# A scan kernel's projections hooked to steps of the second branch, one direction a pass ahead, with B and C spread by DMA

## The reference, cut to what matters

```python
def _mamba(x, Win, convw, convb, Wx, Wdt, bdt, Alog, Dp, Wout):
    xz = x @ Win
    xi, z = jnp.split(xz, 2, axis=-1)
    xi = jax.nn.silu(_causal_dwconv(xi, convw, convb))
    xdbc = xi @ Wx                                  # 8 + 16 + 16 columns
    dt_in, Bm, Cm = ...
    dt = jax.nn.softplus(dt_in @ Wdt + bdt)
    A = -jnp.exp(Alog)
    y = _selective_scan(xi, dt, A, Bm, Cm, Dp)      # h = exp(dt A) h + dt u B;  y = sum_s h C + u D
    return y * jax.nn.silu(z) @ Wout
...
x = layernorm(x + two_directional_mamba(x))         # mamba forward and backward, norms, a small FFN
x = layernorm(x + gated_ffn(x))                     # a*b, two 512x512 layers with gelu, 512 to 128
x = layernorm(x + attention(x))                     # 8 heads, 2 KV heads, latent 32, causal
x = layernorm(x + mixture_of_8_experts(x, top 2))
```

## Time and profile before

| | |
|---|---|
| median of 3 runs | 2261.87 us (2260.26 to 2264.23) |
| the profiled execution | 2270.57 us, its span 2268.8 us |
| busy PE, DVE, ACT, POOL | 1876.0, 1533.2, 1075.0, 791.3 us |
| granted TensorE clock, mean | 0.894 |

### The profile page before, as it was taken

How to read it: one execution, slowest core, us unless ns; L and a number is a source line. 1 busy time by engine, 2 the same in 40 slices (tenths; PEclk the granted TensorE clock), 3 DMA queues, 4 the chain that set the end, 5 groups by cost and what they waited for, 6 DMA issues and landing times.

```text
span 2268.8 us, 28172 instructions
## 1 busy us (share of the span) xinstructions
PE 1876.0 (83%) x8672; PEld 870.7 (38%) x8672; DVE 1533.2 (68%) x2151; ACT 1075.0 (47%) x1486; POOL 791.3 (35%) x632
## 2 busy tenths in 40 slices
PE   5432988899788988899788987899888997897888
PEld 2200334443334434353344433353344433443435
DVE  2988288856798378874888468882888567982214
ACT  2332573537445473546545473545735374452122
POOL 0445053432445044441545133540534324450001
PEclk9555999899899998899899998999998998988999
DMA  6987386706675195824866085823867067740000
GB/s 196 232 204 181 74 215 158 182 15 159 171 187 118 41 213 151 194 49 111 205 166 154 6 217 135 215 70 89 205 161 181 11 161 172 187 111 5 0 1 5
DMA packets 102673, 301.18 MB, mean 133 GB/s; under 512 B 15216, under 2 KB 31232, under 8 KB 102528
## 3 DMA queue, kind: packets, MB, share of 16 engines
q1 hardware_dynamic: 98304, 297.20, 53.7%
q10 hardware_dynamic: 4224, 2.10, 0.3%
HBM read 280.39 MB, written 18.87 MB: 132 GB/s over the span
## 4 chain that ended last, share of the span: by engine, by line
PE 56%; DVE 16%; issue 9%; ACT 8%; DMA 7%; POOL 3%; SPq 1%; DVEq 1%; POOLq 0%; ACTq 0%
PE ps_pair L659 22%; PE ps_in L582 8%; PE ps_pair L756 7%; DVE sb_hst L1197 6%; PE ps_pair L744 5%; PE ps_pair L823 5%; DMA sb_ring<-spread_dram 4%; DMA spread_dram<-sb_dd 2%; PE ps_y L611 2%; POOL sb_hc L1405 2%; PE ps_pair L777 2%; DVE ps_in L1190 2%; PE ps_y L582 2%; ACT sb_ring L891 1%; PE ps_pair L759 1%
## 5 line engine op out<-in xcount | busy, mean ns | idle before, releaser
L1405 POOL TENSOR_TENSOR sb_hc<-sb_hst,sb_crep 128x512 f32<-128x512 f32 x512 | 655.3, 1282 | 721.7 <-DVE sb_hst L1197 700.5
L1197 DVE TENSOR_TENSOR_SCAN sb_hst<-sb_ring,ps_in 128x512 f32<-128x512 f32 x512 | 620.3, 1213 | 0.0
L891 ACT ACTIVATE sb_ring<-sb_ring,sb_A 128x512 f32<-128x512 f32 x512 | 350.9, 714 | 271.1 <-DMA sb_ring<-spread_dram 269.9
L1190 DVE TENSOR_TENSOR ps_in<-sb_ring,ps_brow 128x512 f32<-128x512 f32 x512 | 354.8, 693 | 18.0 <-PE ps_y L582 4.1
L611 PE MATMUL ps_y<-sb_hc,sb_const 128*32 128x512 f32 x1024 | 154.6, 679 | 131.5 <-POOL sb_hc L1405 121.5
L659 PE MATMUL ps_pair<-sb_xn,sb_ew 128*128 128x512 f32 x512 | 251.5, 638 | 8.6 <-DVE sb_h L1349 7.3
L744 PE MATMUL ps_pair<-sb_h,sb_g 128*128 128x512 f32 (+3 forms) x512 | 197.9, 525 | 29.3 <-DVE sb_nmax L1297 28.1
L1395 POOL TENSOR_TENSOR sb_dd<-sb_dd,sb_texp 128x512 f32<-128x512 f32 x32 | 40.8, 1274 | 506.5 <-ACT sb_dd L880 506.5
L853 ACT ACT_TABLE_LOAD x164 | 210.4, 1283 | 3.6 <-PEq L1457 0.8
L756 PE MATMUL ps_pair<-sb_g,sb_h 128*128 128x512 f32 x320 | 185.0, 707 | 16.4 <-ACT sb_sq L1007 9.6
L659 PEld LDWEIGHTS ps_pair<-sb_xn,sb_ew 128*128 128x128 f32 x512 | 99.0, 203 | 137.4 <-issue 108.2
(11 more groups left out here) (223 smaller groups left out, 2312.2 us busy)
## 6 DMA issues: line engine op xcount, KB each, us to landing
sb_ring<-spread_dram SPq DMA_DIRECT2D x512, 512.0 KB, 6.5
spread_dram<-sb_dd SPq DMA_DIRECT2D x32, 512.0 KB, 2.6
...
```

Source lines behind the costliest of these rows:

```text
L891: act.activation(ring[:, n % RING, 0, :], ring[:, n % RING, 0, :], ACT.Exp, scale=A[d][:, g:g + 1]).then_inc(sem["dA"], 1)
L1190: dve.tensor_tensor(ps_in[n % 2][:], ring[:, n % RING, 1, :], ps_brow[:], ALU.mult).then_inc(sem["dbu"], 1)
L1197: dve.tensor_tensor_scan(hst[:, n % 3, :], ring[:, n % RING, 0, :], ps_in[n % 2][:], 0.0, ALU.mult, ALU.add).then_inc(sem["scan"], 1)
L1405: pool.tensor_tensor(hc[:, n % 6, :], hst[:, n % 3, :], crep[n // NU][:], ALU.mult).then_inc(sem["hc"], 1)
```

## The change

The slots of PREP are gone: a pass has 64 slots, one for each unit. The head is cut into pieces that are hooked to steps of `rest`: those of direction 1 to steps 0, 1 and 2 of the same pass, those of direction 0 of the next batch to `fo`, `ao`, `var5` and `x3`. The last unit's scan, its reduction and the last gate go over into slots 0, 2 and 3 of the next pass, and `mo0` follows from slot 4 on. dt of direction 0's first half is made in slots 54 and 55 of the pass before, that of its second half in slots 4 and 5. dtin, B and C come from one product with 40 rows (`x0`, `x1`); SP writes the 32 rows of B and C to `cut_dram` and reads each back with every row repeated 8 times (two 256 KB broadcasts for each direction); DVE copies B to `ps_brow` in both directions. The head uses the banks g0 to g3 of `rest`. The state buffer `hst` has 4 places instead of 3, direction 0's gated output has a buffer of its own, and the result goes out from `xn`, so that the squares of `mo0` do not wait for the store any more. The loop has 6 passes, and the last overlapped pass stands apart, without the pieces of direction 0.

```diff
-PREP, UNITS = 10, 2 * NU
+UNITS = 2 * NU
 RING = 8
-SLOTS = PREP + UNITS + 4
-DT_SLOTS = ((5, 6), (PREP + 1, PREP + 2), (PREP + 22, PREP + 23), (PREP + 38, PREP + 39))
-GATES = (21, 37, 53, UNITS + 3)
+WRAP_SCAN, WRAP_REDUCE, WRAP_GATE = 0, 2, 3
+DT_SLOT = {1: (4, 5), 2: (22, 23), 3: (38, 39), 4: (54, 55)}
+GATE_SLOT = {21: 0, 37: 1, 53: 2}
+HEAD = [["xT"], ["xi00", "xi01"], ["z00", "z01"], ["x0"], ["xi10", "xi11"], ["z10", "z11"], ["x1"]]
+HEAD_PIECES = {"zero": HEAD[:4], "one": HEAD[4:], "keep": [[]]}
+HOOKS = {0: ("one",), 1: ("one",), 2: ("one",), 6: ("keep",), STEP["fo"]: ("zero",), STEP["ao"]: ("zero",),
+         STEP["var5"]: ("zero",), STEP["x3"]: ("zero",)}
...
-PREP_FOLLOW = [1, 1, 1, 1, 1, 1, 1, 1, 2, 2]
+WEIGHT = dict(mo0=5.3, var0=2.0, ff0=1.8, mo2=2.6, var2=1.0, mo3=1.8, var3=1.0, a0=2.0, b0=2.0, a2=2.0, b2=2.0, fo=3.6, var4=1.0,
+              q0=3.1, k=1.6, mT=0.8, ao=1.8, var5=1.0, x3=1.5)
+    steps, k, done = [0] * (WRAP_GATE), 0, 0.0
+    each = sum(cost) / (UNITS - WRAP_GATE)
...
     for steps in steps_of_slot:
-        next(mamba)
+        next(units)
         for _ in range(steps):
             next(rest)
+            for name in hooks.get(k, ()):
+                next(pieces[name])
+            k += 1
...
+                def keep_cut(row, d):
+                    made, b_out, c_out = count(row, "xd", d + 1), count(row, "brep", 16 * d), count(row, "crep", 16 * d)
+                    sp.wait_ge(sem["xd"], made)
...
+                    sp.dma_start(cut[d], xd[64 * d + R:64 * d + R + 2 * S, :]).then_inc(sem["cut"], 16)
+                def load_cut(row, d):
...
+                    sp.dma_start(brep[:], cut[d, 0:S, :].unsqueeze(1).broadcast_to([S, CU, T])).then_inc(sem["brep"], 16)
+                    sp.wait_ge(sem["hc"], c_free)
+                    sp.dma_start(crep[d][:], cut[d, S:2 * S, :].unsqueeze(1).broadcast_to([S, CU, T])).then_inc(sem["crep"], 16)
...
+                    elif n == 18:
+                        keep_cut(at(0), 1)
+                    elif n == 22:
+                        load_cut(at(0), 1)
+                    elif n == 58 and nxt:
+                        keep_cut(at(1), 0)
+                    elif n == 61 and nxt:
+                        load_cut(at(1), 0)
...
-                def dt_in(d):
-                    product(f"dtin{d}", [wx[d][:, h, 0:R] for h in range(NH)], [u[d][:, h, :] for h in range(NH)],
-                            slice(32 * d, 32 * d + R))
-                    product(f"B{d}", [wbc[d][:, h, 0, :] for h in range(NH)], [u[d][:, h, :] for h in range(NH)])
-                    product(f"C{d}", [wbc[d][:, h, 1, :] for h in range(NH)], [u[d][:, h, :] for h in range(NH)])
+                product(f"x{d}", [wx[d][:, h, :] for h in range(NH)], [u[d][:, h, :] for h in range(NH)],
+                        slice(64 * d, 64 * d + R + 2 * S))
...
+            def units(at, prev, nxt):
+                for n in range(UNITS):
...
+                    drive(at(0), n)
+                    if n >= 1:
+                        scan(at(0), n - 1)
+                    elif prev:
+                        scan(at(-1), UNITS - 1)
+                    if n in GATE_SLOT:
+                        gate(at, 0, GATE_SLOT[n], prev)
+                    elif n == WRAP_GATE and prev:
+                        gate(at, -1, 3, prev)
```

More of the change, by code:

```diff
@@ L16 @@
+import itertools
 from contextlib import ExitStack
@@ L163, in rest_uses @@
         elif step == "up":
[L164 removed]
+            uses += [[(f"eb{e}{c}", "eh", 2 * e + c + 1) for c in range(2)]]
         else:
[L166 to L179 removed]
@@ new lines, in place, with later @@
+def place(uses, before):
+    placed, last = {}, dict(before)
+    for name, banks, freed in uses:
+        waits = list(dict.fromkeys(last[bank] for bank in banks if last[bank]))
+        placed[name] = banks, waits, REST_INDEX[name] if name in REST_INDEX else HEAD_INDEX.get(name)
+        last.update({bank: freed for bank in banks})
+    return placed, last
+def later(last):
+    return {bank: freed and (freed[0], freed[1] if freed[2] > -1 else PER[freed[0]], freed[2] - 1) for bank, freed in last.items()}
@@ L209, in follow @@
-def follow():
-    w = FREE
-    rest = [0, 0] + [w["ff"]] * 2 + [w["ln"]] * 3 + [w["ab"]] * 4 + [w["g"]] * 9 + [w["ln"]] + [w["q"]] * 2
-    rest += [w["s"]] * MAXIMA + [w["ln"]] + [w["e"]] * (len(ROUNDS) + 1)
-    rest += [w["ff"]] + [w["ln"]] + [w["lg"]] + [w[step] for step, _ in expert_steps()] + [w["end"]] * 2
-    steps, k = list(PREP_FOLLOW), sum(PREP_FOLLOW)
-    each = sum(rest[k:]) / (SLOTS - PREP)
-    done = 0.0
-    for n in range(SLOTS - PREP):
+        return 4.4
+    return dict(ea=2.0, eb=2.0, eo=1.9, en=1.0)[name[:2]]
@@ L220, in follow @@
+def follow():
+    pieces = {name: iter(HEAD_PIECES[name]) for name in HEAD_PIECES}
+    cost = [weight(k) + sum(PIECE[piece[0]] for hook in HOOKS.get(k, ()) for piece in [next(pieces[hook])] if piece)
+            for k in range(len(REST))]
+    steps, k, done = [0] * (WRAP_GATE), 0, 0.0
+    each = sum(cost) / (UNITS - WRAP_GATE)
+    for n in range(UNITS - WRAP_GATE):
         steps.append(0)
-        while k < len(rest) and (done + rest[k] / 2 <= each * (n + 1) or n == SLOTS - PREP - 1):
-            done += rest[k]
+        while k < len(cost) and (done + cost[k] / 2 <= each * (n + 1) or n == UNITS - WRAP_GATE - 1):
+            done += cost[k]
@@ L652, in done, with rest @@
+            def rest(at, tab):
+                row, claim = at(-1), claim_of(at, tab)
                 def done(ins):
```

773 lines of the change are left out of this document (426 added, 347 removed).

## The result

| | before | changed |
|---|---|---|
| median | 2261.07 us (2259.59 to 2264.23) | 2386.16 us (2384.09 to 2389.97) |
| profiled span | 2268.8 us | 2388.2 us |
| mean granted clock | 0.894 | 0.880 |

The ratio is 1.0553, with a 95% interval of 1.0535 to 1.0571. Slower, as forecast, but by 125 us where the forecast had 61, and 6 us above the upper end of its range.

A forecast was written before the change was run, and what follows sets the result against it. The chain of `rest` on PE, with the head's products in its holes, sets the pass: 14.9 + 42.7 + 212.9 = 270.5 us. Seven passes +75, ends -14, -8.3, +7.3 give 2328.8 us span, 2321.9 us time; range 2255 to 2380.

The forecast's parts named there:

- the waits taken as gone: From `a0` to the next turn: 10 of 15.1 us of waits a pass would go, with ends 0 and 15.1.
- the turn: From the last expert product to `mo0`: PE waits 14.9 us for DVE's work and the gate, in place of 1.75.
- the first batch: Up to the last scan of batch 0: +7.3 us for more DVE work, with bounds -5 and +15.
- four units 7.4: Between the last expert product and `mo0`: four drives and scans on DVE ahead of the gate, 7.4 us.
- `mo0` to `a0`: From `mo0` to the gated FFN's first product: 42.7 us against 47.2 before, with ends 37 and 47.
- ACT's delays: Between `mo0` and `a0`: ACT late behind `xi`, +1.6 us, and table loads around `z`'s silus, +1.9 us.
- `a0` to the turn: From the gated FFN's first product to the last expert product: 212.9 us, from a base of 210.8.
- The other ends: Last overlapped pass -14 us without direction 0's pieces, dt product and dt on DVE; flush -8.3 us.
- The clock's rival: After the idle turn the clock stays low for `mo0`, `mo1` and `xi`, +9 us net; 2385 us, 10% chance.
- Thinner units: Units cost almost nothing from `a0` to the next turn, 202.3 us there; a pass 259.9, total 2248 us, 15% chance.
- SP's queue: New waits in SP's DMA queue make the ring late around unit 60, some 7 us a pass; 2371 us, 5% chance.
- The work removed counts: The turn costs nothing and a pass loses the 7.4 us of B and C products; 2201 us, 5% chance.

The follow-up runs named there:

- e7_gate_slot0: The changed kernel with the leftover reduction and the last gate in slot 0 instead of slots 2 and 3; 2380.57 us (1.0538 of the kernel before).
- e6_late_first: The changed kernel with direction 0's second head in the first batch three to four units later; 2379.09 us (1.0536 of the kernel before).
- e3_before_cut: The kernel before with only the 40-row product for dt's input, B and C and its DMAs; 2213.0 us (0.9781 of the kernel before).

## Why the prediction was right and wrong

The direction and the wait that decides were right; the sum was 64 us short (2321.9 against 2386.2). Three terms failed: the waits taken as gone in the second stage (10 of 15.1 us, found 2.3), the loop's jump at the turn (not in the sum, found 1.99 us at a turn) and the first batch (+7.3, found +22.3). The parts follow in the prediction's order.

**The turn: right mechanism, 4 us short.** Forecast 14.9 us, found 18.8. Its largest term, "four units 7.4", was 7.3. What failed is above all a term that the sum does not have, the loop's jump on DVE: 1.99 us. The rest is small: POOL's read-out ahead of the result's last sum (5.8 us to the end of the norm where 5.2 was taken), the gate's second operation (1.57 us where 0.78 was taken, beside three of POOL's read-outs; in `e7_gate_slot0`, with none beside it, 0.69), and the dt product at the lower clock. That takes 2.07 us and ends 0.5 us behind the gate, where the forecast had put +0.3 and in another term.

**`mo0` to `a0`: 2.5 us too long.** Forecast 42.7, found 40.2. Of what was added for ACT's delays (+1.6 and +1.9) little came, and the clock was 0.92 where the flush, the base of the sum, had 0.80.

**`a0` to the turn: the term that failed is the relief.** Forecast 212.9, found 217.5. The prediction took "10 of them as gone" of 15.1 us of waits, on the ground that units were thinner. Found: PE's idle time in the stage is 28.9 us, in the pass of the earlier trace rows it was 31.2, so 2.3 went, and even that depends on the pass: over six passes of the kernel before it was 26.4 to 31.2. The wait of 4.19 us at the gate went indeed, and 6.30 stood up ahead of the scores, on the same engine's lateness behind dt, seen through POOL's queue. The experts' stage was 59.3 us against 52.5, as forecast (+5 for units and +1.8 for `x0`), with DVE busy 86% of it and not over 90%. With 68 slots the stage is 209.0: the wrap cost there too, which the prediction did not consider at all. How it does so is open: 4.6 of the 8.5 us are waits and 4.0 are clock.

**The first batch: the term was a third of its size.** Forecast +7.3, with a bound at +15; found +22.3, beyond the bound. DVE's busy time rose by 5.7 us, most of the stated items (dt 5.2, copies 2.1). What the sum put at nothing is DVE's idle time, 16.7 us more: 7.6 us for `x0` of the next batch, which `e6_late_first` took away, and 6.2 us of waiting for dt's second half from 66.7 us on, where the kernel before waited 1.5.

**The other ends were right:** last overlapped pass -12.4 (forecast -14), flush -8.0 (forecast -8.3).

Together: 7 x (16.7 - 10.7) = 42, the first batch 15, the last pass 1.6, which is the 59 us between 2328.8 and 2388.2 of span; 4.9 more lie in how the profiled execution stands to the median.

**The rivals.** The clock's rival gave 2385 us, nearly the measured time, by another road: it had `mo0`, `mo1` and xi at the lower level for 12 us; only the reduction (1.93 us), the dt product and `mo0` were (`mo1` 1.02 us at 1090.33). By the Trainium skill, TensorE: Matmul & The Clock Gate, section "Part 1: The HAM clock gate", the clock falls after idle and comes back with sustained work. The trace agrees at this turn: behind 11.98 us of idle the reduction took 1.93 us, where it is 1.07 at the full clock, and `mo0`'s two products 3.56; `mo1`'s took 1.88. Thinner units did not pay for the turn: no second stage of a full pass came under 204 us, not even with 68 slots. SP's queue was nothing, as forecast: behind 65 us no drive of the changed kernel waited for the ring's DMAs. "The work removed counts" was right as to its size, 7.0 us a pass in `e3_before_cut`, but not that it would decide. And for table loads, 208 in place of 164 in the run at 1.28 us, no drain was seen either, as the prediction had decided: one that starts at 1054.64 is followed by an ACTIVATE at 1055.94, 0.02 us behind its end.

**Two sums of the rivals are off.** A second stage of 204 us makes a pass of 261.6 us, not 261.9, and a pass of 252.4 us gives 2195 us with the same ends, not 2201. The forecast and its range do not hang on either.
